# VectorE takes one low part of the probabilities in eight in the last two chunks, GpSimd the others

## The reference

```python
x = L0_attn_x                                        # (1, 2048, 512)
x = x + attn(layernorm(x))
x = x + ffn(layernorm(x))

def attn(x):                                         # 8 groups of 4 query heads, head size 64
    y = x * rsqrt(mean(x * x) + 1e-6) * rms_w
    q, k, v = split(y @ w_in.T)                      # 32 query heads, 8 key heads, 8 value heads
    q, k = rope(q), rope(k)
    qk = where(causal, q @ k.T * 64 ** -0.5, -inf)
    return x + (softmax(qk) @ v) @ w_out.T

def ffn(x):                                          # weights rounded to -s, 0, s with s = mean(abs(w))
    return (silu(x @ wg.T) * (x @ wu.T)) @ wd.T
```

## Time and profile before

| what | value |
|---|---|
| median of 3 runs | 2113.49 us |
| the profiled execution's own time | 2111.11 us |
| its span, first to last instruction | 2109.2 us |
| PE busy | 1950.0 us (92%) |
| GpSimd (POOL) busy | 1585.6 us (75%) |
| VectorE (DVE) busy | 1247.0 us (59%) |
| ScalarE (ACT) busy | 930.1 us (44%) |
| low parts on GpSimd, L818 | 1280, 1136.7 us, mean 916 ns |

### The profile page before, as it was taken

The page is one execution under the profiler, slowest core; times in us unless marked ns, Lnnn a source line. Parts: engine busy times, 40 slices in busy tenths (PEclk is TensorE's granted clock), DMA queues, the critical chain, the costliest instruction groups (busy, mean ns, idle before and its releaser), DMA issues. The chain is left out here.

```text
span 2109.2 us, 55361 instructions
## 1 busy us (share of the span) xinstructions
PE 1950.0 (92%) x21382; PEld 1182.9 (56%) x21382; DVE 1247.0 (59%) x3158; ACT 930.1 (44%) x1985; POOL 1585.6 (75%) x1803
## 2 busy tenths in 40 slices
PE   2599999999999999999999999999969898999998
PEld 1256666666666666666666666666634444444443
DVE  8568757757765774776587477657626662221221
ACT  3245555555555555555555555555631211111110
POOL 5479999999999999999999999999943441221211
PEclk9889999999999999999999999999989999999999
DMA  5332234224223322322432232332245530000000
GB/s 173 130 77 47 46 67 66 46 60 74 47 47 69 74 44 50 72 47 48 79 68 45 47 74 42 52 77 52 37 145 199 206 109 1 10 10 20 5 15 21
DMA packets 301573, 137.05 MB, mean 65 GB/s; under 512 B 248208, under 2 KB 285328, under 8 KB 299792
## 3 DMA queue, kind: packets, MB, share of 16 engines
q1 hardware_dynamic: 301328, 133.69, 27.1%
HBM read 49.74 MB, written 25.17 MB: 36 GB/s over the span
## 5 line engine op out<-in xcount | busy, mean ns | idle before, releaser
L818 POOL TENSOR_TENSOR pl<-p 128x512 f16<-128x512 f32 (+3 forms) x1280 | 1136.7, 916 | 51.1 <-ACT p L671 50.3
L671 ACT ACTIVATE p<-a_ps 128x512 f32<-128x512 f32 (+3 forms) x1280 | 672.8, 532 | 630.9 <-PE a_ps L604 393.7
L741 DVE TENSOR_REDUCE mpart<-a_ps 128x1 f32<-128x512 f32 x768 | 518.2, 687 | 139.5 <-PE a_ps L588 133.5
L620 PE MATMUL a_ps<-v,p 128*128 128x65 f16 x4352 | 528.4, 193 | 30.0 <-POOL pl L818 25.4
L622 PE MATMUL a_ps<-v,p 128*128 128x64 f16 x4352 | 531.0, 194 | 0.0
L624 PE MATMUL a_ps<-v,pl 128*128 128x65 f16 x4352 | 528.0, 192 | 0.0
L620 PEld LDWEIGHTS a_ps<-v,p 128*128 128x128 bf16 x4352 | 412.3, 97 | 149.5 <-ACT p L671 39.2
L588 PE MATMUL a_ps<-k_hl,q_hh 128*128 128x512 f16 (+3 forms) x1280 | 440.2, 349 | 32.2 <-issue 8.9
L622 PEld LDWEIGHTS a_ps<-v,p 128*128 128x128 bf16 x4352 | 406.2, 98 | 99.6
L604 PE MATMUL a_ps<-q_lm,k_h 128*128 128x512 f16 (+3 forms) x1280 | 445.4, 348 | 0.0
L603 PE MATMUL a_ps<-q_hh,k_hl 128*128 128x512 f16 (+3 forms) x1280 | 444.6, 347 | 0.0
(11 more groups left out here) (97 smaller groups left out, 2443.3 us busy)
## 6 DMA issues: line engine op xcount, KB each, us to landing
attn_scratch<-o_turn SPq DMA_DIRECT2D x64, 256.0 KB, 3.0
p_att<-attn_scratch SPq DMA_DIRECT2D x32, 512.0 KB, 4.4
raw<-ffn_t SPq DMA_DIRECT2D x12, 1024.0 KB, 4.9
wraw<-w_in_t SPq DMA_DIRECT2D x8, 768.0 KB, 5.4
resid_scratch<-xin SPq DMA_DIRECT2D x4, 1024.0 KB, 4.3
raw<-w_out_t SPq DMA_DIRECT2D x1, 4096.0 KB, 14.6
x<-resid_scratch SPq DMA_DIRECT2D x4, 1024.0 KB, 7.7
out<-x SPq DMA_DIRECT2D x16, 256.0 KB, 2.0
```

The costliest lines, as they stand in the source:

```text
L620: nc.tensor.matmul(o, weights, v[:, par, j, 0:VU], start=(j == 0 and t == 0), stop=False, skip_group_check=True)
L671: nc.scalar.activation(p32[:, i % RING, r * P:CHUNK], sbank(i)[:, r * P:CHUNK], ACT.Exp, scale=SCALE).then_inc(exp_done, 1)
L741: nc.vector.reduce_max(mpart[:, u % 2, t, kk:kk + 1], bank, AX.X).then_inc(maxs_used, 1)
L818: nc.gpsimd.tensor_tensor(pl[:, i % RING, cols], p32[:, i % RING, cols], p_high[:, i % RING, cols], ALU.subtract).then_inc(low_ready, 1)
```

## The change

The low parts of steps with `j % 8 == 5` in chunks 2 and 3 are computed by VectorE. That is `j` = 5 in the four units of chunk 2, and `j` = 5 and `j` = 13 in the four units of chunk 3, 12 steps a group: 53, 65, 77, 89, 101, 109, 117, 125, 133, 141, 149 and 157. Over 8 groups it is 96 of the 1280 low parts. Those with `j` = 13 (109, 125, 141 and 157) lie on the diagonal. GpSimd computed 384 columns for them, VectorE computes all 512. VectorE does the low part of step `i` in its iteration `i + 2`, behind the first piece of slot `i + 1` and ahead of everything else of that iteration, and waits for `exp_done`. The one semaphore `low_ready` becomes two, one for each engine, and TensorE waits for the one that belongs to the step.

```diff
+LOW_LAG = 2
+
+
+def low_by_dve(i):
+
+    u, j = step_of(i)
+    return u // HG >= 2 and j % 8 == 5
...
+DVE_STEPS = [i for i in range(STEPS) if low_by_dve(i)]
+POOL_STEPS = [i for i in range(STEPS) if not low_by_dve(i)]
...
-        low_ready = sem("low_ready")
+        low_dve = sem("low_dve")
+        low_pool = sem("low_pool")
...
-                    pe.wait_ge(low_ready, g * STEPS + i + 1)
+                    if low_by_dve(i):
+                        pe.wait_ge(low_dve, g * len(DVE_STEPS) + DVE_STEPS.index(i) + 1)
+                    else:
+                        pe.wait_ge(low_pool, g * len(POOL_STEPS) + POOL_STEPS.index(i) + 1)
...
+                def low_part(i):
+                    dve.wait_ge(exp_done, g * STEPS + i + 1 + EXP_AHEAD)
+                    nc.vector.tensor_tensor(pl[:, i % RING], p32[:, i % RING], p_high[:, i % RING], ALU.subtract)\
+                        .then_inc(low_dve, 1)
+
...
-                for n in range(len(part) + 1):
+                for n in range(len(part) + LOW_LAG):
                     step, _, pieces = slot(part, n - 1)
                     for piece in pieces[:1]:
                         reduce_piece(*piece)
+                    if slot(part, n - LOW_LAG)[0] in DVE_STEPS:
+                        low_part(slot(part, n - LOW_LAG)[0])
...
-                                            ALU.subtract).then_inc(low_ready, 1)
+                                            ALU.subtract).then_inc(low_pool, 1)
...
-                        if step >= HEAD:
+                        if step >= HEAD and step in POOL_STEPS:
                             low_part(step)
```

## The result

The changed kernel takes 2130.7 us (median of 6 runs, 2129.82 to 2133.02) against 2113.11 (6 runs). The ratio is 1.0086, with a 95% interval of 1.0073 to 1.0099: slower by 18 us, where 2116.4 was forecast and 2123 was the upper end. The profiled execution's own time is 2132.01 us and its span 2130.2, 21.0 more than before.

The account below looks back on a forecast made before the run. TensorE was taken to bound slots 48 to about 145, GpSimd each group's end. Groups 0 to 6 lose 0.8 us each (+5.6), the last gains 2.7: +2.9 on 2113.5 gives 2116.4 us, range 2106 to 2123.

Parts of the forecast that it names:

- TensorE is the bound up to slot 145: Groups 0 to 6: TensorE bounds slots 48 to about 145, GpSimd the last fifteen steps; GpSimd's time is worth nothing before.
- The price of a moved part: Each moved low part: VectorE 0.685 us if GpSimd is idle, at most 1.58; costs GpSimd 0.45 by taking turns.
- Loss at step 65, 1.35, and at step 101, 0.35: Groups 0 to 6: VectorE reads a bank late, so TensorE loses 1.35 us at step 65 and 0.35 at 101.
- The other eight moved steps at nothing: Moved steps up to 145 besides 65 and 101: the banks have enough time and VectorE idles, so no cost.
- The last group, -2.7: Last group: GpSimd bounds the end from about step 130, so freed time shortens it by 2.7 us.
- The gain is 0.55 + 0.34 = 0.9 us a group: End of groups 0 to 6: steps 149 and 157 free 0.55 and 0.34 us of GpSimd, all of it gained.
- The sign that I had named: In the profile after, PE's wait for GpSimd's low-part line should fall from 25.4 us.
- The first: Rival: VectorE late in more places, side-work banks in slots 53 to 125, +7 on top, 2123 us; chance 0.29.
- The case without a lock: Rival: VectorE's new part takes 0.685 us and nothing from GpSimd; -12.2, 2101.3 us; chance 0.06.

Follow-up runs that it names:

- The kernel with one SBUF input: The changed kernel with the 96 moved low parts left out, VectorE taking a maximum over the same 512 columns instead: 2106.5 us, ratio 0.9958.
- The two kernels with fillers: The changed kernel plus three unused matmuls of 252 columns per step, in a group's last five steps (2128.4 us) or in steps 153 to 156 (2122.1 us).
- the one without the last unit's steps: The changed kernel with steps 149 and 157 back on GpSimd, steps 53 to 141 staying on VectorE: 2124.1 us, ratio 1.0054.
- the kernel of nine steps without fillers: The changed kernel with steps 65, 101 and 157 back on GpSimd and no added matmuls: 2107.6 us, ratio 0.9981.
- the first of these kernels: The changed kernel plus three unused matmuls of 252 columns in each of the last five steps of a group: 2128.4 us.

## Why the prediction was wrong, point by point

- **TensorE is the bound up to slot 145.** Right: none of the time that GpSimd was freed of ahead of slot 144 shortened a stretch of groups 0 to 6.
- **The price of a moved part.** Right. VectorE took 0.69 to 1.62 us, mean 1.14 (foreseen 0.68 to 1.58, near 1.1); GpSimd's next one 1.48. At step 149 VectorE came first and waited for nothing (0.69), and GpSimd's next took 1.56, 0.52 more. The kernel with one SBUF input shows that it is the sharing.
- **Loss at step 65, 1.35, and at step 101, 0.35.** Right: 1.38 and 0.35 to 0.36.
- **The other eight moved steps at nothing.** Right: no stretch of theirs grew.
- **The last group, -2.7.** Near: -2.5 behind its first sixteen slots. The two kernels with fillers, whose clock doesn't fall near that end, differ there by 3.0.
- **"The gain is 0.55 + 0.34 = 0.9 us a group."** This step failed. I followed GpSimd's chain to its last low part and took that for TensorE's end. In groups 0 to 6 TensorE's last wait there is for step 156. The time that step 157 frees comes behind it, while its turn on the shared inputs lengthens GpSimd's low part of step 155 (1.486 us at 845.86) by 0.45. Measured were 0.45 a group for step 149 alone and 0.04 for both: 7 x 0.9 = 6 us that weren't there. I held the gain against the stretch's total wait of 2.4 us, but didn't see which low part each piece of it was for. The sign that I had named came: TensorE's wait for GpSimd's low parts, which should have fallen from 25.4 us, is 26.0.
- **Left out: TensorE's clock.** The prediction has no term for it. One fall at a group's end before, seven after, 1.3 to 1.7 us each: some 8 to 9 us more. In the changed kernel the falls start between the last two pauses, in the last one or within 0.3 us behind it, and the first of these two grew from 0.47 to 0.92 us because step 157's turn came ahead of step 155. The fillers show the price. Why the clock fell at all seven ends stays open: the kernel with steps 149 and 157 alone had three falls, and the one without the last unit's steps two with the old pauses. The seven falls begin 184.3 us apart, one at every end. The four of the kernel with one input begin 361.8 us apart, at every second end. What sets that rhythm isn't shown.
- **The sum.** +2.9 was forecast. 6 us of missing gain and 8 to 9 us of clock make it 17 to 18, and 17.6 was measured.
- **The rivals.** None had the cause. The first had the right sign, but for a place (slots 53 to 125) where nothing was lost beyond the forecast. The case without a lock (2101.3 us) is refuted for two inputs. One input gave 2106.5, with four falls of about 1.5 us in it.

## What to carry to other kernels

Before a chain is credited with a gain, name the last link that the next engine waits for; time freed behind it is worth nothing, and its side effects fall ahead of it. When work goes from one of two engines that take turns to the other, the price is a wait of either, so it belongs where the receiving engine has a break and, as far as these runs go, where the giving one isn't in a dense stream. If the bound engine pauses already at a place, look at its granted clock there before the pauses are made longer.

## What the runs showed that I had not expected

- VectorE can miss its turn. In the earlier trace rows and in the changed kernel it waited for one GpSimd instruction, at most two. In variants with fewer moved parts it waited for 4 to 9 in a row: 9.25 us twice, 5.64, 5.77, and with step 157 alone 4.1 in five of eight and 5.13 in one. The Trainium skill (SBUF — State Buffer, section "SBUF: two separate sides") has whichever starts first keep the shared pair for the whole instruction, and the other blocked. It doesn't say who goes next, and I had taken one wait as the limit. By the traces it isn't. Three missed turns began 0.05 to 0.06 us ahead of a GpSimd start, but in the kernel of nine steps without fillers one that began 0.06 us ahead was served after 1.65 us. Those of step 157 began 0.42 us into a GpSimd instruction, as did the one at 845.28 above, which was served. What decides is open.
- A fall of the clock to 1.2 GHz lasted 3.4 us wherever it came at a group's end, and over all kernels it took 1.1 to 1.7 us from TensorE. About 0.3 us of filler matmuls in each of four steps (five in the first of these kernels) kept it away in all four kernels that had them. Where TensorE paused anyway they cost nothing that could be measured.
